# The value product of an attention kernel with both halves of the values side by side, in a new order of the batch

## The reference, cut to what matters

```python
x = x + tanh(g_xattn[0]) * L0_xattn(layernorm(x), ctx)   # 16 heads of 64, 112 queries, 375 keys
x = x + tanh(g_ffn[0])   * L0_ffn(layernorm(x))          # a 256x256 mix
x = x + tanh(g_xattn[1]) * L1_xattn(layernorm(x), ctx)   # one head of 256
x = x + tanh(g_ffn[1])   * L1_ffn(layernorm(x))          # 16 experts, 4 a token

# L0_xattn
q = (xn @ w_q).reshape(B, SQ, NUM_HEADS, DIM_HEAD)
k, v = jnp.split(context @ w_kv, 2, axis=-1)
scores = jnp.einsum('bqhd,bkhd->bhqk', q * SCALE, k)
attn = jax.nn.softmax(scores, axis=-1)
out = jnp.einsum('bhqk,bkhd->bqhd', attn, v)             # the value product
out = out.reshape(B, SQ, INNER) @ w_out + b_out
```

## Time and profile before

| | |
|---|---|
| median of three runs | 1104.79 us |
| the profiled execution | 1109.83 us, span 1108.1 us |
| PE busy | 1039.2 us (94%), 7055 matmuls |
| VectorE busy | 803.5 us (73%) |
| ScalarE busy | 714.7 us (65%) |
| GpSimd busy | 516.6 us (47%) |
| granted TensorE clock, mean | 0.977 |

### The profile page before, as it was taken

How to read it: one execution, slowest core, us unless ns; L and a number is a source line. 1 busy time by engine, 2 the same in 40 slices (tenths; PEclk the granted TensorE clock), 3 DMA queues, 4 the chain that set the end, 5 groups by cost and what they waited for, 6 DMA issues and landing times. The chain is left out here.

```text
span 1108.1 us, 22305 instructions
## 1 busy us (share of the span) xinstructions
PE 1039.2 (94%) x7055; PEld 961.0 (87%) x7055; DVE 803.5 (73%) x2017; ACT 714.7 (65%) x1853; POOL 516.6 (47%) x628
## 2 busy tenths in 40 slices
PE   5899999999999999999999999999998778889995
PEld 4899899999989999999999999999997758879983
DVE  4646787868787777778786868787776765866665
ACT  4645767676767767676767676766765545646650
POOL 3413345464554546454646454554644224574450
PEclk9989999999999999999999999999999889989998
DMA  5332122222323232322222222222113522344379
GB/s 179 101 96 70 43 51 71 57 68 56 83 61 80 57 82 58 78 66 51 66 59 69 52 72 59 58 57 68 50 46 96 182 54 89 123 162 149 134 211 288
DMA packets 79840, 98.46 MB, mean 89 GB/s; under 512 B 14939, under 2 KB 71901, under 8 KB 79728
## 3 DMA queue, kind: packets, MB, share of 16 engines
q1 hardware_dynamic: 70400, 80.08, 27.1%
q0 software_dynamic: 8784, 16.96, 4.5%
q10 hardware_dynamic: 544, 0.00, 0.0%
HBM read 41.98 MB, written 23.03 MB: 59 GB/s over the span
## 5 line engine op out<-in xcount | busy, mean ns | idle before, releaser
L942 POOL TENSOR_TENSOR prob<-prob,rinv 112x750 f32<-112x750 f32 x128 | 184.1, 1438 | 251.1 <-DVE rinv L1614 250.7
L1032 ACT ACTIVATE prob<-ps_s,negmax 112x375 f32<-112x375 f32 x256 | 144.0, 570 | 59.7 <-DVE negmax L1608 56.9
L1621 DVE TENSOR_TENSOR pT_lo<-ps_pt,pT_hi 125x672 fp32r<-125x672 f32 x128 | 108.6, 848 | 64.1 <-ACT pT_hi L1169 64.1
L1712 PE MATMUL ps_kv<-ctxT_hi,wkv 128*128 128x376 f32 x512 | 138.4, 351 | 2.4 <-DVE v_lo L1281 1.2
L1608 DVE TENSOR_REDUCE negmax<-ps_s 112x2 f32<-112x750 f32 x128 | 119.0, 930 | 4.4 <-PE ps_s L1960 4.3
L1712 PE MATMUL ps_kv<-wkv,ctxT_hi 128*125 128x512 f32 x384 | 111.5, 413 | 1.1 <-DVE k_low L1277 0.2
L1022 ACT ACTIVATE v_hi<-ps_kv 125x512 fp32r<-125x512 f32 x96 | 57.3, 597 | 82.9 <-PE ps_kv L1712 82.9
L1970 PE MATMUL ps_pt<-ident,prob 112*125 112x112 f32 x768 | 104.4, 273 | 2.3 <-POOL prob L942 2.3
L901 POOL DMA_INDIRECT places<-ysb,place_i x72 | 71.6, 994 | 71.7 <-ACT ysb L1105 59.7
L1169 ACT ACTIVATE pT_hi<-ps_pt 125x672 fp32r<-125x672 f32 x128 | 93.6, 731 | 7.0 <-PE ps_pt L1970 1.1
L1960 PE MATMUL ps_s<-kx,qx_hi 128*112 128x376 f32 x256 | 94.1, 367 | 3.5 <-DMA kx<-k_low 2.6
(11 more groups left out here) (312 smaller groups left out, 2715.4 us busy)
## 6 DMA issues: line engine op xcount, KB each, us to landing
kx<-k_low SPq DMA_DIRECT2D x256, 94.0 KB, 2.2
xg<-rows_by_expert SPq DMA_DIRECT2D x72, 128.0 KB, 2.0
qx_hi<-qx_hi SPq DMA_DIRECT2D x64, 112.0 KB, 2.3
zb<-places SPq DMA_DIRECT2D x16, 448.0 KB, 13.9
ctx_in<-in_ctx SPq DMA_DIRECT2D x16, 375.0 KB
stage_w<-in_L_ffn_mlp_w SPq DMA_DIRECT2D x16, 256.0 KB, 5.0
arena<-in_L_ffn_mlp_w SPq DMA_DIRECT2D x16, 256.0 KB, 6.1
stage_w<-in_L_xattn_w_kv SPq DMA_DIRECT2D x4, 512.0 KB, 9.4
```

The source lines that it names most:

```text
L942: e_prob.done(eng.tensor_tensor(prob[0:TQ, p % 2, :, :], prob[0:TQ, p % 2, :, :], rinv[:, 2 * p:2 * p + 2].unsqueeze(2).broadcast_to([TQ, ...
L1032: e_exp.done(eng.activation(prob[0:TQ, p % 2, half, :], S[0:TQ, half, 0:SK], ACT.Exp, bias=negmax[:, h:h + 1], accum_out=rowsum[:, h:h + 1]))
L1621: e_pt_lo.done(eng.tensor_tensor(pT_lo[:, :, :, :].rearrange("p h k t -> p h (k t)"), PT[0:KEYT, :, 0:NKEY * TQ], pT_hi[:, :, :, :].bitcas ...
L1712: last = eng.matmul(out_, lhs(i, k), rhs(j, k), start=(n == 1), stop=(n == KT * len(PASSES)))
```

## The change

The high and low parts of a head's values now lie side by side in one tile `vx`, and the high and low parts of the transposed weights in one tile `pTx`. One matmul multiplies both parts of one head's values by both parts of its weights: six matmuls a pair instead of nine. Its four blocks are summed afterwards: ScalarE copies one block to `o_sum` and one to `oT`, VectorE adds the third to `o_sum`, giving `o_add`, and GpSimd adds `o_add` to `oT`. The order of the groups is new, `n1` and `n2` are made a slot later on VectorE (except in the last batch), the comparison for the routing moves behind the groups, `xn` is made a slot later, and `base_row` shares its place with `xm`, so that GpSimd waits for the store of the row before. Two quarters of `w_kv` are loaded from ScalarE's queue in slot -4 instead of SyncE's.

```diff
-        v_hi = t("v_hi", [128, NKEY, INNER], F32R)
-        v_lo = t("v_lo", [128, NKEY, INNER], F32R)
+        vx = t("vx", [128, NKEY, NH, 2, DH], F32R)
...
+        pTx = t("pTx", [KEYT, 2, 2, NKEY, TQ], F32R)
+        pT_hi, pT_lo = (pTx[:, n, :, :, :] for n in range(2))
...
-        KV_AT = (("v", 1, 0), ("x", 0, -5), ("k", 2, 1), ("q", 0, -3), ("r", 0, 36), ("k", 7, 10),
-                 ("v", 3, 6), ("q", 1, 3), ("v", 4, 9), ("c", 0, -5), ("c", 1, -4), ("k", 5, 7),
-                 ("k", 0, -3), ("v", 2, 2), ("e", 0, 39), ("k", 4, 5), ("v", 5, 10), ("k", 6, 9),
-                 ("k", 3, 3), ("k", 1, -1), ("v", 0, -1))
+        KV_AT = (("q", 1, 0), ("v", 1, 1), ("k", 2, 1), ("v", 2, 2), ("k", 3, 3), ("r", 0, 36), ("k", 4, 5),
+                 ("v", 3, 5), ("k", 5, 7), ("e", 0, 39), ("v", 4, 8), ("k", 6, 9), ("x", 0, -6), ("v", 5, 10),
+                 ("k", 7, 11), ("c", 0, -5), ("c", 1, -4), ("q", 0, -4), ("k", 0, -3), ("k", 1, -1), ("v", 0, -1))
...
-        AT_LN, AT_XN, AT_XB0 = -10, -8, 3
+        AT_LN, AT_XN, AT_XB0 = -10, -7, 3
@@ SyncE
-            for n, half in ((0, 0), (2, 1), (1, None), (3, None)):
+            for n, half in ((0, 0), (2, 1)):
@@ GpSimd
-                        eng.wait_ge(kv_dve, KV_LO[KV_USE["e", 0, tb.off - 1] + 1])
+                        eng.wait_ge(f_base, 16 * tb.off)
...
+                for p in range(NP):
+                    st = due(g, AT_O[p] + 1)
+                    if st:
+                        e_o_sum.wait_ge(eng, st, p + 1)
+                        e_oT.done(eng.tensor_tensor(oT[:, p, :], oT[:, p, :], o_add[:, :], ALU.add))
@@ ScalarE
+                if g == AT_SPLIT[0]:
+                    for n in (1, 3):
+                        eng.dma_start(w_kv_part(w_kv_in, n), w_kv_part(w_kv.rearrange("(k p) n -> p k n", p=128), n)
+                                      ).then_inc(ld_wkv[n], 16)
...
                             e_o.wait_ge(eng, st, p + 1)
+                            e_o_sum.wait_ge(eng, st, p)
+                            eng.activation(o_sum[:, :, :], O_ALL[64:128, :, 0, :], ACT.Copy)
                             for half in range(2):
-                                rows_ = slice(64 * half, 64 * half + 64)
-                                last = eng.activation(oT[rows_, p, :], OT[rows_, half * TQ:(half + 1) * TQ],
+                                last = eng.activation(oT[64 * half:64 * half + 64, p, :], O_ALL[0:64, half, 1, :],
                                                       ACT.Copy)
-                            e_oT.done(last)
+                            e_o_act.done(last)
@@ VectorE
-                tb = due(g, 20)
+                tb = also(g, 21, 20)
                 if tb:
                     e_rs_t.wait_ge(eng, tb, 1)
                     normed(tb, 0)
-                tb = due(g, 22)
+                tb = also(g, 23, 22)
...
+                tb = due(g, 34)
+                if tb and tb is not BATCH[B - 1]:
+                    compare(tb)
                 tb = due(g, 35)
                 if tb:
+                    if tb is not BATCH[B - 1]:
+                        rank(tb)
...
+                        e_o_act.wait_ge(eng, st, p + 1)
+                        e_oT.wait_ge(eng, st, p)
+                        for half in range(2):
+                            last = eng.tensor_tensor(o_add[64 * half:64 * half + 64, :], O_ALL[0:64, half, 0, :],
+                                                     o_sum[:, half, :], ALU.add)
+                        e_o_sum.done(last)
@@ PE
                         e_pt_lo.wait_ge(eng, st, p + 1)
-                        e_oT.wait_ge(eng, st, p)
-                        n = 0
-                        for i, j in PASSES:
+                        e_o_sum.wait_ge(eng, st, p)
+                        for half in range(2):
                             for k in range(NKEY):
-                                n += 1
-                                last = eng.matmul(OT[:, 0:2 * TQ].rearrange("p (h t) -> p h t", t=TQ),
-                                                  vv[i][0:KEYT, k, p * 128:(p + 1) * 128],
-                                                  pT[j][:, :, k, :], start=(n == 1),
-                                                  stop=(n == NKEY * len(PASSES)))
+                                last = eng.matmul(O_ALL[:, half, :, :],
+                                                  vx[0:KEYT, k, 2 * p + half, :, :].rearrange("p j d -> p (j d)"),
+                                                  pTx[:, :, half, k, :], start=(k == 0), stop=(k == NKEY - 1))
```

More of the change, by code:

```diff
@@ L460, in program @@
         e_o = event("e_o", NP)
+        e_o_act, e_o_sum = event("e_o_act", NP), event("e_o_sum", NP)
         e_oT = event("e_oT", NP)
@@ L487, in program @@
         qk = (qk_hi, qk_lo)
-        vv = (v_hi, v_lo)
-        pT = (pT_hi, pT_lo)
+        v_heads = vx[:, :, :, :, :].rearrange("p k h j d -> p k j h d")
+        O_ALL = OT[:, 0:4 * TQ].rearrange("p (h j t) -> p h j t", h=2, j=2)
         AT_S = [2 * p for p in range(NP)]
@@ L629, in _ @@
             load_ctx(0)
-            for n, half in ((0, 0), (2, 1), (1, None), (3, None)):
+            for n, half in ((0, 0), (2, 1)):
                 load(w_kv_part(w_kv_in, n), w_kv_part(wide(w_kv), n), ld_wkv[n])
-                if half is not None:
-                    load(wq[:, :, half * 512:(half + 1) * 512], wide(w_q)[:, :, half * 512:(half + 1) * 512], ld_wq[half])
+                load(wq[:, :, half * 512:(half + 1) * 512], wide(w_q)[:, :, half * 512:(half + 1) * 512], ld_wq[half])
             for n, g in enumerate((g_xattn, g_ffn)):
@@ L1021, in projection @@
                 if kind == "v":
-                    ins = eng.activation(v_hi[0:KEYT, n % NKEY, n // NKEY * 512:(n // NKEY + 1) * 512],
-                                         bank[0:KEYT, :], ACT.Copy)
+                    heads = slice(n // NKEY * NP, (n // NKEY + 1) * NP)
+                    ins = eng.activation(v_heads[0:KEYT, n % NKEY, 0, heads, :],
+                                         bank[0:KEYT, :].rearrange("p (h d) -> p h d", d=DH), ACT.Copy)
                 ins.then_inc(kv_act, 1)
@@ L1121, in _ @@
                 if g % 2 == 0:
-                    for p in range(NP):
-                        st = due(g, AT_O[p] + 1)
-                        if st:
-                            e_o.wait_ge(eng, st, p + 1)
-                            for half in range(2):
-                                rows_ = slice(64 * half, 64 * half + 64)
-                                last = eng.activation(oT[rows_, p, :], OT[rows_, half * TQ:(half + 1) * TQ],
-                                                      ACT.Copy)
-                            e_oT.done(last)
                     tail(g)
@@ L1279, in projection @@
                 if kind == "v":
-                    at = slice(n // NKEY * 512, (n // NKEY + 1) * 512)
-                    ins = eng.tensor_tensor(v_lo[0:KEYT, n % NKEY, at], bank[0:KEYT, :],
-                                            v_hi[0:KEYT, n % NKEY, at].bitcast(F32), ALU.subtract)
+                    heads = slice(n // NKEY * NP, (n // NKEY + 1) * NP)
+                    ins = eng.tensor_tensor(v_heads[0:KEYT, n % NKEY, 1, heads, :],
+                                            bank[0:KEYT, :].rearrange("p (h d) -> p h d", d=DH),
+                                            v_heads[0:KEYT, n % NKEY, 0, heads, :].bitcast(F32), ALU.subtract)
                 ins.then_inc(kv_dve, 1)
@@ L1321, in normed, with compare, rank @@
                                            ALU.subtract, ALU.mult))
+            def compare(tb):
+                e_tl.wait_ge(eng, tb, 11)
+                e_tl_dve.done(eng.tensor_tensor(gl[:, :], TL[0:TQ, 0:NE], gbrow[0:TQ, :], ALU.add))
+                e_tl_dve.wait_ge(eng, tb, TL_READ[10][1])
+                e_gmax.done(eng.tensor_reduce(rs[:, 0:1], gl[:, :], AX.X, ALU.max, negate=True))
+                g_j = gl[:, :].unsqueeze(1).broadcast_to([TQ, NE, NE])
+                g_e = gl[:, :].unsqueeze(2).broadcast_to([TQ, NE, NE])
+                ct(eng.tensor_tensor(cmp_b[:, :, :], g_j, g_e, ALU.is_equal))
+                ct(eng.tensor_tensor(cmp_a[:, :, :], g_j, g_e, ALU.is_gt))
+            def rank(tb):
+                ct.wait_ge()
+                ct(eng.tensor_tensor(cmp_b[:, :, :], cmp_b[:, :, :], earlier[0:TQ, :, :], ALU.mult))
+                ct.wait_ge()
+                ct(eng.tensor_tensor(cmp_a[:, :, :], cmp_a[:, :, :], cmp_b[:, :, :], ALU.add))
+                ct.wait_ge()
+                ct(eng.tensor_reduce(rk[:, 0, :], cmp_a[:, :, :], AX.X, ALU.add))
+                ct.wait_ge()
+                e_seen.wait_ge(eng, tb, 0)
+                e_mask.done(eng.tensor_scalar(mask[:, :], rk[:, 0, :], TOPK - 0.5, None, ALU.is_lt))
             def tail_first(g):
```

41 lines of the change are left out of this document (11 added, 30 removed).

## The result

The changed kernel took 1224.21 us, median of four runs (1220.64 to 1230.92), beside 1105.34 for the kernel before (1103.99 to 1107.68): ratio 1.108 [1.102, 1.114]. The forecast had the sign right and half the size: 1162 us, with a range that ended at 1188.

What follows compares the result with a forecast made beforehand. PE was taken to bound the steady middle: 48.65 us of own work plus 7.0 of waits, 55.65 a batch, +56.4 over fourteen; with +0.1, +1.3 and -0.6, 1167.0 profiled, median 1162 us. Range 1100 to 1188.

Steps and rivals of the forecast that it cites:

- PE's own work: Steady batch on PE: 51.62 us less 2.68 for fewer matmuls and 0.29 for a wait, 48.65 us.
- The places of the waits: Eight places: tail step 1, step 2, v4, c1 with q0, step 7, v5, v2, q1; 0.35 to 1.64 us each.
- The sum of the waits: PE's waits on its readers at eight places of the new order, added: 7.0 us a batch.
- step 1's chain: From v3 to tail step 1: copy, v_lo and norm take 2.33 us against PE's 0.69; wait 1.64.
- about 9 if all readers also lag: Upper bound on PE's waits a batch, if all readers lag as behind an odd slot of VectorE; lower bound 4.3.
- What the sums cost: Per pair: ScalarE's copy 0.26 us, VectorE's two additions 0.37, GpSimd's addition 0.5; busy sums stay under PE's 48.65.
- points 5 to 8: Waits ahead of step 7 (0.96 us), v5 (0.6), v2 (0.35) and q1 (0.8), from readers working in written order.
- That `prob` is hidden: GpSimd's `prob` comes up to 1.8 us later, but PE needs it two slots on; uncovered, up to 1 us a pair.
- the saving of 2.68 us: Three of nine value matmuls fewer a pair, 0.335 us, times eight pairs: 2.68 us a batch off PE.
- rival A: Readers keep up at all eight wait places and PE stays the bound: 47.5 us less, 1057 us; chance 0.12.
- Rival C: Clock falls to half in pauses at tail steps 1 and 2: 1.5 us lost a batch, 1183 us; chance 0.12.
- Start, batch 0, the end: Outside the steady batches: start -0.6 us (between -1.8 and +2), batch 0 +0.1, last batch +1.3.

Runs made afterwards that it cites:

- a set at 1105: Group of runs beside the unchanged kernel before, which takes 1105 us there; in the other kind of set it takes 1131 to 1135 us.

## Why the prediction was right or wrong

**PE's own work: right.** 59.07 less 11.0 of waits is 48.1 us, 48.65 forecast. The value matmuls are 768 and 0.111 apart, as the row of the kernel before had them.

**The places of the waits: right, eight of eight.** Of the signs that were named, PE is idle before step 1 on `n12t` and before step 2 on `nT`, and waits for k_low ahead of v4 and c1. The others went wrong: batches are not of 55.6 us, VectorE and ScalarE are busy for 4.5 and 3.5 us more a batch and not 3 and 2, and the granted clock under 1 in the middle, named as a sign of being wrong, is there.

**The sum of the waits, 7.0 us: the step that failed.** It measured 11.0, and 4.0 x 14 = 56 us is nearly the whole miss. Three errors are in it.
- The chains were begun with readers that are free, or with the order before as a guide to how late they are. They were not free: in step 1's chain ScalarE began 0.39 us late, still at k4, and all eight places came out longer, by 0.10 to 0.64. Without the sums step 1's bracket is 1.65 instead of 2.05, so 0.4 of its 0.57 is the sums'; v4's is 1.00 with and without them. The bound "about 9 if all readers also lag" was the right thought, and 2 us too low.
- The ninth place, the routing group (0.88), was left out. The runs have it only with the sums and the new order together.
- "What the sums cost" set 0.26 us for the copy (0.37 measured) and 0.37 for the two additions (0.55), since it took an overlap of 0.1 us for all neighbours; the two 64x112 copies of the earlier trace rows, 0.52 long with the next start 0.54 behind the first, show none. It priced the sums in points 5 to 8 alone, and took the busy sums, 43 and 39 us under PE's 48.65, as the test whether they cost anything more. They came to 44.6 and 40.3, and cost 0.056 of the time in the old order (0.038 in a set at 1105, with nine matmuls and without GpSimd's part), 0.033 in the new. That handoffs go from PE to ScalarE to VectorE and back to PE is not tested by busy shares. That `prob` is hidden fits the traces, in which PE does not wait for it in batches 4 to 11; no run tests it.

**That the saving of 2.68 us counts in full: wrong, and not seen as a risk.** In the old order only 1.0 us of it reached the end, without any sums; rival A rested on all of it, and no run comes near its 1057 us. The Trainium skill ("Perfetto Trace Analysis", "Identifying the Most-Contended Engine") says to optimize the engine of highest occupancy first and warns that matmul busy share is no measure of distance from the roofline. PE had the highest by far, and 5% less work on it brought 0.013 of the time: here the next bound lay one microsecond a batch behind it.

**Rival C, the clock: right in kind.** It was the forecast and 14 x 1.5 us on top, 1183 us. The clock fell in half the steady batches, not in all, at 1.6 us each (60.3 against 58.7), 0.8 us on the mean; so C's price for one fall was right, and its total is too low by the same waits as the forecast's. The rule cited with it (the Trainium skill, "TensorE: Matmul & The Clock Gate", "The HAM clock gate") agrees with the trace, in which PE was busy for 1.24 of 3.43 us before a fall. The batches without a fall had the same waits, so here the rule does not tell which batch is hit.

**Start, batch 0, the end: wrong together by 9.** -0.6 forecast for the start, +2.6 measured: ScalarE issued the two loads from 9.17 to 11.12 and split its first quarter at 11.17, where before that was at 9.54, 1.6 us earlier. The other 1.0 us was not traced.

```profile
9.17 1.95 ACTq L1128 DMA_DIRECT2D stage_w<-in_L_xattn_w_kv  x2
11.17 1.06 ACT L996 ACTIVATE wkv<-stage_w 128x1024 fp32r<-128x1024 f32 x1 [1.52 <-issue]
```

Batch 0 was given +0.1 and took 3.7, the end +1.3 and took 3.7.

In sum, the batch shown: forecast 55.65, +4.0 of waits and -0.6 of own work give its 59.07; this closes by itself, since own work was taken as what the waits leave. The mean of 59.63 is 0.56 above it, for the batches with a fall of the clock.

## What to carry to other kernels

That an engine is busy for 94% of the time says nothing of how far behind the next bound is. Here a kernel with 0.3 us of waits a batch had readers that came just in time, and 2.7 us less work on PE brought 1.0. Before taking work off the busiest engine, walk its handoffs as a loop over the engines and add the new work to that loop, however idle each engine is. And a wait taken away at one place of such a loop can come back at the next, as step 1's came back at v4: price a removed wait by the run without it, not by its length.
